# Attention row maxima per 128 queries: thin scores in four 32-row groups and one wide maximum, with compact reciprocals

## The chip, the cores and the metric

The kernel runs on one core of a Trainium2 chip. The metric is the device time of one execution in microseconds (us); lower is better. Engines are named as in the profile: PE is TensorE (PEld its weight loads), DVE is VectorE, ACT is ScalarE, POOL is GpSimd, SP is SyncE, whose queue here issues nearly all DMAs.

## The reference, cut to what matters

It is a transformer block with conditioning: two sequences of 2048 rows of 512 features, 16 heads of 32 features, an MLP of width 1024, all float32.

```
ada = silu(c) @ Wada + bada             # six shift / scale / gate rows per sequence
h = ln(x) * (1 + scale_msa) + shift_msa
q, k, v = h @ Wq + bq, h @ Wk + bk, h @ Wv + bv        # 16 heads of 32
A = softmax(q @ k.T / sqrt(32))         # per sequence and head: 2048 x 2048
x = x + gate_msa * ((A @ v) @ Wo + bo)
h2 = ln(x) * (1 + scale_mlp) + shift_mlp
out = x + gate_mlp * (gelu(h2 @ W1 + b1) @ W2 + b2)
```

The softmax needs, for each of the 2048 queries of a head, a number near the row's largest score to subtract before the exponential; any such number gives the same quotient.

## The kernel before, in words

There are three stages on one core: the first computes q, k and v for 8 chunks of 512 rows and writes them to DRAM; the second is attention, one head after another, 2 x 16 = 32 heads (numbered g = 0 to 31); the third is output projection and MLP, again by chunks. The change is in the second stage.

Products that need accuracy split each float32 number into a leading part (`hi`, rounded to the type float32r) and a remainder (`lo`). For the scores, 32 features of a head are stacked three times over 96 partitions: q as hi, hi, lo and k as hi, lo, hi, so one matmul over 96 rows gives hi·hi + hi·lo + lo·hi. These stacks are `qs[u]` and `ks[u]`. Row 96 (`M_ROW`) of `qs` carries minus the row maximum of each query, row 96 of `ks` ones, so a matmul over 97 rows gives scores less the maximum.

A head is worked in 16 steps (`NT`), step t for keys 128t to 128t+127. In one step PE computes the four pieces of transposed scores (128 keys x 512 queries, `scores`, line 1113), ACT exponentiates each (line 670) into `prob`, a ring of four steps, and PE then multiplies with v (`values`, line 1127: four column groups of 32, each an ordinary float32 matmul that stands as two instructions, hence x8 in the trace). The sums over the keys (the softmax's denominators) are made in two ways: the tiles in `POOL_TILES` are added up by POOL in halves of 1024 columns (line 538) into `psum_acc`; the others (`PE_TILES`, 5 of 16) and `psum_acc` at the end are summed by PE with a matrix of ones (`tile_sum`, `finish_denominators`, line 1118, x8 each). ACT copies the finished denominators of head g-1 out in step 1 of head g (line 650); DVE inverts them over 128 x 512 elements (line 874), scales the output (line 877), and SP stores it (line 398).

Between these, in a fixed order written out by hand (`FILLS_AT`, `SPREAD`), PE computes for the *next* head another 64 pieces of scores, queries on the partitions, 512 keys each, over 96 rows (`max_scores`, line 1104), in a ring of three PSUM banks; DVE takes the maximum of each (line 868) into `part_max`. After the 64th, DVE reduces the 64 columns to 16 (line 812), PE transposes them (line 1047), DVE negates them (line 818), and SP puts them into row 96 (`put_max`, line 391). The scores of the head use a second ring of three banks.

Each engine runs its list in order and waits on semaphores. In SP's list `stage2(g)` waits for the denominators of head g-1, loads q, k and v of head g+2 (`load_head`: seven DMAs of 256 KB, v last, in 2048 runs of 128 bytes), then `put_max(g+1)`, then `store_head(g-1)`. Three buffers (`NBUF`) hold q, k, v and output of a head. The first head's maxima are found in the first stage.

Of the kernel before, what the change touches and what calls it, by code (L numbers as in the profile page):

```python
# [19 lines left out]
F32 = mybir.dt.float32  # L20
# [5 lines left out]
P = 128  # L26
# [17 lines left out]
NBUF = 3  # L44
M_ROW = 3 * DH
POOL_TILES = [0, 1, 2, 3, 5, 6, 7, 9, 10, 11, 12]
# [4 lines left out]
FILLS_AT = (5, 5, 4, 4, 5, 4, 5, 4, 4, 5, 5, 4, 4, 4, 2, 0)  # L51

SPREAD = {0: (0, 0, 0, 0, 0), 2: (1, 1, 0, 0, 0), 4: (1, 1, 0, 1, 1), 5: (1, 1, 1, 1, 1)}
STEP_MAX = NT - 2
A_BANKS, B_BANKS = 3, 3
# [3 lines left out]
STEPS_SPLIT, STEP_PROJECT, STEP_ROOT, STEP_TRANSPOSE = (2, 4), 6, 10, 15  # L59
AHEAD = 3  # L60
COL = P // 4
LOADS = 7


def block_kernel(nc, x, cT, wq, wk, wv, wo, w1, w2, wada, bqT, bkT, b1T, badaT, bada, bv, bo, b2, out):
# [3 lines left out]
    att_dram = nc.dram_tensor("attention_T", [D, B * L], F32, kind="Internal").ap()  # L69

    with ExitStack() as ctx:
# [28 lines left out]
        qs = [view(acts_r, 4096 * u, L) for u in range(NBUF)]  # L100
        ks = [view(acts_r, 4096 * u + L, L) for u in range(NBUF)]

        oT_r = view(acts_r, 0, 2, KC, CH)
        g_r = view(acts_r, 4096, 4, 2, CH)
        h2T = view(acts_r, 8192, 2, KC, CH)
        assert [g % NBUF for g in range(G - 3, G)] == [2, 0, 1]
# [7 lines left out]
        v_sb = [view(work, at, NT, DH) for at in (512, 0, 1024)]  # L114
        o_st = [view(work, at, CH) for at in (2560, 3072, 1536)]
# [30 lines left out]
        row_max = sb("row_max", [P, NT])  # L146
        neg_max = sb("neg_max", [NT, P], F32R)
# [46 lines left out]
        ones_row = sem("ones_row")  # L194
        head_in = [sem(f"head_in{u}") for u in range(NBUF)]
        a_mm = sem("a_mm")
        a_max = sem("a_max")
        max_ok = sem("max_ok")
        maxT_mm = sem("maxT_mm")
        neg_ok = sem("neg_ok")  # L200
        neg_in = sem("neg_in")
# [6 lines left out]
        den_raw = sem("den_raw")  # L208
        rec_ok = sem("rec_ok")
        o_ok = sem("o_ok")  # L210
# [33 lines left out]
        def rows_of(w, c0):  # L244
# [8 lines left out]
                    for n, (w, at) in enumerate(((wq, stage[0]), (wk, stage[1]), (wv, as_piece(gate))))]  # L253
        w_pieces += [(w2[n * D:(n + 1) * D, :].rearrange("(k p) n -> p k n", p=P), stage[n],
                      [w2_r[:, s, n * KC:(n + 1) * KC, :] for s in range(2)]) for n in range(2)]
# [4 lines left out]
        LATE_STEP = 2  # L260
# [24 lines left out]
        def _(sp):  # L285
# [101 lines left out]

            def put_max(g, u):

                sp.wait_ge(neg_ok, g + 1)  # L390
                sp.dma_start(qs[u][M_ROW:M_ROW + 1, :].bitcast(F32),
                             neg_max[:].bitcast(F32)).then_inc(neg_in, 16)
# [23 lines left out]
            load_head(1, 1)  # L416
# [4 lines left out]
            for k, (rows, _) in enumerate(late):  # L421
# [6 lines left out]
                if k == 1:  # L428
                    sp.wait_ge(qkv_mm, NCHUNK * MM_CHUNK)
                    stored(NCHUNK)  # L430
                    load_head(2, 2)
            put_max(1, 1)
            with sp.Fori(0, G // NBUF - 1) as i:
                for k in range(1, NBUF + 1):
                    stage2(i * NBUF + k, k % NBUF, True)
# [19 lines left out]
            for g in range(G // NBUF * NBUF - NBUF + 1, G - 1):  # L455
                stage2(g, g % NBUF, g + 2 < G)
# [3 lines left out]
            load_x(0, 0, xc, xc_in)  # L460
            store_head(G - 2, (G - 2) % NBUF)
            load_first_oT(1)
# [31 lines left out]
        def _(pool):  # L494
# [14 lines left out]
            def row_of_ones(u):  # L509
                nc.gpsimd.memset(ks[u][M_ROW:M_ROW + 1, :].bitcast(F32), 1.0).then_inc(ones_row, 1)  # L510
                pool.wait_ge(ones_row, u + 1)

            row_of_ones(0)
# [8 lines left out]
            for u in range(1, NBUF):  # L522
                row_of_ones(u)
# [42 lines left out]
        def _(act):  # L566
# [91 lines left out]
            def probs(g, u, uses, prev, between={}):  # L658


                for t in range(NT):
# [6 lines left out]
                    for j in range(NQ):  # L668
                        act.wait_ge(b_mm, g * (NT * NQ) + t * NQ + j + 1)
                        nc.scalar.activation(prob[:, t % RING, j * CH:(j + 1) * CH], ps[:, A_BANKS + (u + t * NQ + j) % B_BANKS, :],  # L670
                                             ACT.Exp, scale=SCALE).then_inc(exp_ok, 1)
                    if prev and t == 0:
                        take_output(g - 1, (u + 2) % NBUF, uses)
# [8 lines left out]
            with act.Fori(0, G // NBUF) as i:  # L682
                for k in range(1, NBUF + 1):
                    probs(i * NBUF + k, k % NBUF, i, True)
            def split_first_oT(half):
# [39 lines left out]
        def _(dve):  # L725
            nc.vector.memset(cs_pad, 0.0).then_inc(pad_ok, 1)
            nc.vector.memset(ones[:], 1.0).then_inc(ones_ok, 1)
# [82 lines left out]
            def row_maxima(g):  # L810
                dve.wait_ge(a_max, (g + 1) * FILLS)
                nc.vector.tensor_reduce(row_max[:], part_max[:], AX.X, ALU.max).then_inc(max_ok, 1)

            def negate_max(g):
                dve.wait_ge(maxT_mm, g + 1)
                if not isinstance(g, int) or g:
                    dve.wait_ge(neg_in, g * 16)
                nc.vector.tensor_scalar(neg_max[:], ps[0:NT, 0, 0:P], -1.0, None, ALU.mult).then_inc(neg_ok, 1)
# [3 lines left out]
            def chunk(n, p, turn, nxt=True, nxt2=True, at=T_AT, ada={}, max_after={}, max_at=None):  # L822

                for m in range(MM_CHUNK):
                    for _ in range(max_after.get(m, 0)):
                        first_max(next(fills))
                    if m == max_at:
                        row_maxima(0)
                    take(n, m)
                    if m == max_at:  # L830
# [475 lines left out]
```

## Time and profile before

| | us |
|---|---|
| median of 3 runs (2633.13 to 2639.24) | 2637.26 |
| span of the profiled execution | 2625.2 |
| PE busy | 2543.3 (97%) |
| DVE busy | 1841.4 (70%) |
| POOL busy | 1625.0 (62%) |
| ACT busy | 1309.9 (50%) |

The page gives no time of the profiled execution beside its span; the median of the timed runs is 12.1 us above that span. Attention takes the stretch from about 420 to 2180 us. Busy time of PE counts from a matmul's start to its modelled end, and matmuls overlap, so PE's share is no measure of how much of its peak is used. The columns of the trace's answers are named where each group stands below.

### The profile page before, as it was taken

To read this page: it belongs to the slowest core of one execution; us is meant where nothing else is said; L and a number is where in the kernel's file an instruction comes from. 1 tells how busy PE (TensorE), PEld (TensorE's weight loads), DVE (VectorE), ACT (ScalarE), POOL (GpSimd) and SP (SyncE) were. 2 spreads that over 40 slices of the span, in tenths; PEclk is the share of its full clock that TensorE was granted. 3 is DMA by queue.
4 is the path that set the end of the run, shared out by engine and by line. 5 is a ranking of instruction groups with operands and counts; after the bars stand their busy time and mean duration, and the time that the engine had idled before them with its cause. 6 is when DMAs were issued, how large, how long until landed. Compare 5 with 4: busy or idle time off the path is not lost.

```text
span 2625.2 us, 45742 instructions
## 1 busy us (share of the span) xinstructions
PE 2543.3 (97%) x13208; PEld 1482.7 (56%) x13208; DVE 1841.4 (70%) x2872; ACT 1309.9 (50%) x2429; POOL 1625.0 (62%) x744
## 2 busy tenths in 40 slices
PE   7999899999999999999999999999999979999998
PEld 5788654444444444444444444444444437888887
DVE  5444588887877878778777787778778745555553
ACT  3333245665666656666666665666656642222221
POOL 0000157887888878888878888878888772112120
PEclk9999999999999999999999999999999989999999
DMA  7655631111211112211122111122111001121100
GB/s 263 207 192 167 153 112 49 33 34 39 60 34 33 33 38 56 40 33 33 35 44 56 33 33 35 35 52 46 33 34 33 21 25 53 49 73 71 48 32 32
DMA packets 141459, 163.15 MB, mean 62 GB/s; under 512 B 76048, under 2 KB 92944, under 8 KB 134032
## 3 DMA queue, kind: packets, MB, share of 16 engines
q1 hardware_dynamic: 140480, 159.95, 23.2%
q8 instruction: 129, 2.11, 0.3%
q14 instruction: 130, 1.06, 0.1%
q10 hardware_dynamic: 720, 0.02, 0.0%
HBM read 100.95 MB, written 58.72 MB: 61 GB/s over the span
## 4 chain that ended last, share of the span: by engine, by line
PE 93%; DVE 3%; issue 1%; ACT 1%; DMA 1%; SPq 0%; POOL 0%; ACTq 0%; POOLq 0%; DVEq 0%
PE ps L1113 21%; PE ps L1015 20%; PE ps L1104 19%; PE ps L1127 18%; PE ps L1118 7%; PE ps L1248 7%; DVE part_max L868 1%; PE ps L1024 1%; DVE weights_r L882 1%; PE ps L1059 1%; PE ps L1047 0%; DMA work<-v_rows 0%; DVE work L942 0%; ACT work L670 0%; DMA work<-in_x 0%
## 5 line engine op out<-in xcount | busy, mean ns | idle before, releaser
L538 POOL TENSOR_TENSOR work<-work 128x1024 f32<-128x1024 f32 x640 | 1505.7, 2395 | 296.7 <-PE ps L1118 262.7
L868 DVE TENSOR_REDUCE part_max<-ps 128x1 f32<-128x512 f32 x1984 | 1229.0, 682 | 321.3 <-PE ps L1104 320.7
L670 ACT ACTIVATE work<-ps 128x512 f32<-128x512 f32 x2048 | 1070.9, 602 | 697.3 <-PE ps L1113 697.2
L1113 PE MATMUL ps<-acts_r 97*128 97x512 f32 x2048 | 836.4, 418 | 26.0 <-ACT work L670 14.7
L1104 PE MATMUL ps<-acts_r 96*128 96x512 f32 x1984 | 811.3, 409 | 6.8 <-DVE part_max L868 6.7
L1113 PEld LDWEIGHTS ps<-acts_r 97*128 97x128 f32 x2048 | 383.1, 190 | 396.7 <-ACT work L670 308.4
L1127 PE MATMUL ps<-work 128*32 128x512 f32 x4096 | 545.3, 604 | 0.0
L1104 PEld LDWEIGHTS ps<-acts_r 96*128 96x128 f32 x1984 | 375.6, 189 | 263.0 <-DVE part_max L868 182.4
L1015 PE MATMUL ps<-acts_r,weights_r 128*128 128x512 f32 x1536 | 380.3, 397 | 5.7 <-DVE acts_r L790 5.7
L1015 PEld LDWEIGHTS ps<-acts_r,weights_r 128*128 128x128 f32 x1536 | 291.1, 191 | 69.3 <-issue 6.8
L547 POOL TENSOR_TENSOR work<-work,gate_b 128x512 f32<-128x512 f32 x60 | 84.5, 1439 | 214.3 <-DMA work<-in_x 172.8
L1127 PEld LDWEIGHTS ps<-work 128*32 128x32 f32 x4096 | 94.2, 109 | 203.2 <-issue 186.6
L1118 PE MATMUL ps<-work,ones 128*32 128x512 f32 x1536 | 206.4, 610 | 0.0
L505 POOL TENSOR_TENSOR var_eps<-var_eps,mv 128x4 f32<-128x4 f32 x16 | 3.2, 201 | 327.2 <-DVE mv L768 327.2
L713 ACT ACTIVATE work<-ps,b_sb 128x512 f32<-128x512 f32 x64 | 44.1, 690 | 309.7 <-PE ps L1015 309.6
L1248 PE MATMUL ps<-w_r,acts_r 128*128 128x512 f32 x768 | 184.5, 391 | 0.0
L1015 PE MATMUL ps<-weights_r,acts_r 128*128 128x512 f32 x768 | 183.6, 392 | 0.0
L1015 PEld LDWEIGHTS ps<-weights_r,acts_r 128*128 128x128 f32 x768 | 143.7, 188 | 36.9 <-issue 7.0
L1248 PEld LDWEIGHTS ps<-w_r,acts_r 128*128 128x128 f32 x768 | 143.0, 188 | 29.2 <-issue 0.2
L607 ACT ACTIVATE work<-ps,bq_sb 128x512 fp32r<-128x512 f32 x64 | 44.1, 689 | 206.3 <-PE ps L1015 170.9
L922 DVE CAST acts_r<-work 128x512 fp32r<-128x512 f32 x64 | 27.9, 436 | 128.6 <-ACT work L713 128.6
L874 DVE RECIPROCAL bv_rows<-bv_rows 128x512 f32<-128x512 f32 x32 | 106.6, 3331 | 8.0 <-ACT bv_rows L650 8.0
(69 smaller groups left out, 897.5 us busy)
## 6 DMA issues: line engine op xcount, KB each, us to landing
work<-in_x SPq DMA_DIRECT2D x16, 1024.0 KB, 5.4
acts_r<-q_hi SPq DMA_DIRECT2D x64, 256.0 KB, 4.8
acts_r<-k_hi SPq DMA_DIRECT2D x64, 256.0 KB, 6.4
q_hi<-work SPq DMA_DIRECT2D x32, 256.0 KB, 2.6
q_lo<-work SPq DMA_DIRECT2D x32, 256.0 KB, 3.3
k_hi<-work SPq DMA_DIRECT2D x32, 256.0 KB, 2.6
k_lo<-work SPq DMA_DIRECT2D x32, 256.0 KB, 3.2
v_rows<-work SPq DMA_DIRECT2D x32, 256.0 KB, 2.0
```

The lines of the kernel that those rows point to most:

```text
L538: nc.gpsimd.tensor_tensor(psum_acc[:, at], first, prob[:, t % RING, at], ALU.add).then_inc(add_ok, 1)
L547: nc.gpsimd.tensor_tensor(xc[b][:, t, :], xc[b][:, t, :], gate_b[:, which, b, :], ALU.add).then_inc(done, 1)
L607: nc.scalar.activation(qk_st[:, m % 2, 0, :].bitcast(F32R), ps[:, 2 + m % 4, :], ACT.Identity, bias=bq_sb[:, m // KC, m % KC:m % KC + 1]). ...
L670: nc.scalar.activation(prob[:, t % RING, j * CH:(j + 1) * CH], ps[:, A_BANKS + (u + t * NQ + j) % B_BANKS, :], ACT.Exp, scale=SCALE).then_ ...
L868: nc.vector.tensor_reduce(part_max[:, f // NQ, f % NQ:f % NQ + 1], ps[:, (u + f) % A_BANKS, :], AX.X, ALU.max).then_inc(a_max, 1)
L874: nc.vector.reciprocal(recip[:], recip[:]).then_inc(rec_ok, 1)
L1015: mm = nc.tensor.matmul(o, lhs(s, kk), rhs(r, kk), start=(kk == 0 and s == r), stop=(kk == KC - 1 and s == 1))
L1104: nc.tensor.matmul(ps[:, (u + f) % A_BANKS, :], qs[u][0:M_ROW, f // NQ * P:(f // NQ + 1) * P], ks[u][0:M_ROW, j * CH:(j + 1) * CH], start= ...
L1113: nc.tensor.matmul(ps[:, A_BANKS + (u + t * NQ + j) % B_BANKS, :], ks[u][0:M_ROW + 1, t * P:(t + 1) * P], qs[u][0:M_ROW + 1, j * CH:(j + 1 ...
L1118: mm = nc.tensor.matmul(ps[j * DH:(j + 1) * DH, DEN_BANK, :], ones[:, 0:DH], src(j), start=first, stop=last)
L1127: mm = nc.tensor.matmul(ps[j * DH:(j + 1) * DH, O_BANK, :], v_sb[u][:, t, :], prob[:, t % RING, j * CH:(j + 1) * CH], start=(t == 0), stop ...
L1248: mm = nc.tensor.matmul(ps[:, 4 + t, :], g_r[:, f % 4, s, t * P:(t + 1) * P], w2_r[:, r, f, :], start=(f == 0 and s == r), stop=(f == FB - ...
```

## The change

In words:

- The maximum is taken of hi·hi alone (over 32 rows instead of 96). The 32 rows of q's leading part are loaded four times, into partitions 0-31, 32-63, 64-95 and 96-127 (`qm`), and a quarter of the keys into each (`km`). For 128 queries (a block b), PE issues four matmuls of 32 rows, one per row group, into four PSUM banks (`block_scores`), and DVE takes one maximum over all 2048 columns (`block_max`). There are 16 blocks per head; block t+2 of the next head is issued in step t (`MAX_LEAD` 2). The four banks are one buffer: PE waits for the maximum of block b before it writes block b+1. The scores keep two banks instead of three.
- The 16 columns of maxima are transposed by DVE (32 x 32 blocks), without PE and without a negation (row 96 of `ks` is now minus one); `put_max` takes four DMAs.
- The denominators: SP spreads one row of each quarter to 128 x 16 elements, DVE inverts these, SP writes them to DRAM and reads them back, broadcast to 32 partitions for each quarter. DVE inverts in step 5 and scales the output in step 9 of the next head.
- SP's `stage2` now waits for head g-1's denominators, loads head g+1 (seven DMAs) and then `qm`, `km` of head g+2 (`load_max`, eight DMAs: 4 x 256 KB and 4 x 64 KB), then does the spreading, the store, and `put_max`. Two buffers instead of three.
- POOL adds 9 tiles instead of 11; PE sums 7 instead of 5.
- The order of a step on PE: two scores, the block of maxima, two scores, values of the step before, its tile sum. The last 128 rows of W2 are loaded at the end of attention (their place holds `km`). In the last head the projection starts at step 7 instead of 6.

The core of the diff (`load_max`, `spread_reciprocals` and `stage2` are in SP's list; `transpose_max` to the first `head` in DVE's; `block_scores` and the loop over the steps in PE's):

```diff
-NBUF = 3
+NBUF = 2
-POOL_TILES = [0, 1, 2, 3, 5, 6, 7, 9, 10, 11, 12]
+POOL_TILES = [0, 1, 2, 4, 5, 7, 9, 10, 12]
-A_BANKS, B_BANKS = 3, 3
+MAX_LEAD = 2
+FIRST_PAIRS = (4, 9)
+A_BANKS, B_BANKS = 4, 2
+STEP_RECIP, STEP_SCALE = 5, 9
...
+            def load_max(g, u):
+                r = bass.ds(g * DH, DH)
+                for j in range(NQ):
+                    at = slice(j * DH, (j + 1) * DH)
+                    sp.dma_start(qm[u][at, :].bitcast(F32), qk_hi[0][r, :]).then_inc(max_in[u], 16)
+                    sp.dma_start(km[u][at, :].bitcast(F32), qk_hi[1][r, j * CH:(j + 1) * CH]).then_inc(max_in[u], 16)
...
+            def spread_reciprocals(g):
+                sp.wait_ge(den_raw, g + 1)
+                for j in range(NQ):
+                    sp.dma_start(den_c[j * DH:(j + 1) * DH, :], recip[j * DH:j * DH + 1, :].rearrange("o (p c) -> o p c", c=NT)).then_inc(den_in, 16)
+                sp.wait_ge(rec_ok, g + 1)
+                sp.dma_start(rec_dram.rearrange("(p c) -> p c", c=NT), den_c[:]).then_inc(rec_out, 16)
+                sp.wait_ge(rec_out, g * 16 + 16)
+                for j in range(NQ):
+                    sp.dma_start(recip[j * DH:(j + 1) * DH, :],
+                                 rec_dram[j * CH:(j + 1) * CH].rearrange("(o c) -> o c", o=1).broadcast_to((DH, CH))).then_inc(rec_in, 16)
...
-            def stage2(g, u, load):
-                if load:
-                    sp.wait_ge(den_mm, START + g)
-                    load_head(g + 2, (u + 2) % NBUF)
-                put_max(g + 1, (u + 1) % NBUF)
-                store_head(g - 1, (u + 2) % NBUF)
+            def stage2(g, u, more=True):
+                sp.wait_ge(den_mm, START + g)
+                load_head(g + 1, 1 - u)
+                if more:
+                    load_max(g + 2, u)
+                spread_reciprocals(g - 1)
+                store_head(g - 1, 1 - u)
+                put_max(g + 1, 1 - u)
...
+            def transpose_max(g):
+                if not isinstance(g, int) or g:
+                    dve.wait_ge(m_max, g * NT)
+                    dve.wait_ge(maxT_in, g * (16 * MAX_PIECES))
+                nc.vector.transpose(max_T[:], row_max[:]).then_inc(maxT_ok, 1)
+            def block_max(g, b):
+                if b == 0:
+                    dve.wait_ge(maxT_ok, g)
+                dve.wait_ge(m_mm, (g - 1) * NT + b + 1)
+                nc.vector.tensor_reduce(row_max[:, b:b + 1], ps[:, 0:A_BANKS, :].rearrange("p j n -> p (j n)"), AX.X, ALU.max).then_inc(m_max, 1)
+            def small_reciprocals(g):
+                dve.wait_ge(den_in, g * (16 * NQ) + 16 * NQ)
+                nc.vector.reciprocal(den_c[:], den_c[:]).then_inc(rec_ok, 1)
+            def scale_output(g, u):
+                dve.wait_ge(rec_in, g * (16 * NQ) + 16 * NQ)
+                dve.wait_ge(o_raw, g + 1)
+                nc.vector.tensor_tensor(o_st[u], o_st[u], recip[:], ALU.mult).then_inc(o_ok, 1)
+            def head(g, u, nxt=True, more=True):
+                for t in range(NT):
+                    if t == STEP_RECIP:
+                        small_reciprocals(g - 1)
+                    if t == STEP_SCALE:
+                        scale_output(g - 1, 1 - u)
+                    if nxt and t + MAX_LEAD < NT:
+                        block_max(g + 1, t + MAX_LEAD)
+                    if nxt and t + MAX_LEAD == NT - 1:
+                        transpose_max(g + 1)
+                    if more and t + MAX_LEAD >= NT:
+                        block_max(g + 2, t + MAX_LEAD - NT)
...
+            def block_scores(g, u, b):
+                if not isinstance(g, int) or g > 1 or b:
+                    pe.wait_ge(m_max, (g - 1) * NT + b)
+                for j in range(NQ):
+                    at = slice(j * DH, (j + 1) * DH)
+                    mm = nc.tensor.matmul(ps[:, j, :], qm[u][at, b * P:(b + 1) * P], km[u][at, :], start=True, stop=True)
+                mm.then_inc(m_mm, 1)
...
+                for t in range(NT):
                     scores(g, u, t, 0)
                     scores(g, u, t, 1)
                     if t in between:
                         between[t]()
                     scores(g, u, t, 2)
                     scores(g, u, t, 3)
+                    if t:
+                        values(g, u, t - 1)
+                        if t - 1 in PE_TILES:
+                            tile_sum(g, t - 1)
+                    elif loads is not None:
+                        last_values(g - 1, 1 - u)
+                    if t == 1 and loads is not None:
+                        finish_denominators(g - 1)
```

## Rows read from the trace of the kernel before

**Rows 1.** The page, busy us, share of the span, instructions of each engine.

```profile
PE 2543.3 (97%) x13208; PEld 1482.7 (56%) x13208; DVE 1841.4 (70%) x2872; ACT 1309.9 (50%) x2429; POOL 1625.0 (62%) x744
```

**Rows 2.** Chain of waits through one head, 1087.7 to 1143.9 us: its shares by line.

```profile
by line: PE ps L1113 31.8%; PE ps L1104 28.8%; PE ps L1127 27.4%; PE ps L1118 10.4%; issue 1.7%; PE ps L1047 0.6%
```

**Rows 3.** Timeline, DVE: start us, duration us; the reciprocals of heads 0 and 29.

```profile
477.76 3.33 DVE L874 RECIPROCAL bv_rows<-bv_rows 128x512 f32<-128x512 f32 x1
...
2088.73 3.33 DVE L874 RECIPROCAL bv_rows<-bv_rows 128x512 f32<-128x512 f32 x1
```

**Rows 4.** Timeline, PE, two steps inside a head: start us, duration us, count.

```profile
1097.82 1.06 PE L1118 MATMUL ps<-work,ones 128*32 128x512 f32 x8
1098.70 1.04 PE L1127 MATMUL ps<-work 128*32 128x512 f32 x8
1099.68 0.50 PE L1104 MATMUL ps<-acts_r 96*128 96x512 f32 x1
1100.01 0.40 PE L1113 MATMUL ps<-acts_r 97*128 97x512 f32 x1
...
1101.66 0.40 PE L1104 MATMUL ps<-acts_r 96*128 96x512 f32 x1
1101.99 1.06 PE L1127 MATMUL ps<-work 128*32 128x512 f32 x8
1102.99 0.50 PE L1113 MATMUL ps<-acts_r 97*128 97x512 f32 x1
1103.33 0.39 PE L1104 MATMUL ps<-acts_r 96*128 96x512 f32 x1
```

**Rows 5.** The page, weight loads: busy us, mean ns of one.

```profile
L1104 PEld LDWEIGHTS ps<-acts_r 96*128 96x128 f32 x1984 | 375.6, 189 | 263.0 <-DVE part_max L868 182.4
L1127 PEld LDWEIGHTS ps<-work 128*32 128x32 f32 x4096 | 94.2, 109 | 203.2 <-issue 186.6
```

**Rows 6.** Timeline, DVE, the same head.

```profile
1091.17 0.69 DVE L877 TENSOR_TENSOR work<-work,bv_rows 128x512 f32<-128x512 f32 x1
1103.75 2.48 DVE L868 TENSOR_REDUCE part_max<-ps 128x1 f32<-128x512 f32 x4 [0.47 <-PE ps L1104]
1142.69 0.22 DVE L812 TENSOR_REDUCE row_max<-part_max 128x16 f32<-128x64 f32 x1
```

**Rows 7.** Groups by line, 1000 to 1520 us: busy us, mean ns of one.

```profile
L868 DVE TENSOR_REDUCE part_max<-ps 128x1 f32<-128x512 f32 x604 | 374.1, 683 | 97.4 <-PE ps L1104 97.2
```

**Rows 8.** Timelines, ACT and POOL, the same head.

```profile
1103.52 2.07 ACT L670 ACTIVATE work<-ps 128x512 f32<-128x512 f32 x4 [0.52 <-PE ps L1113]
...
1099.09 47.04 POOL L538 TENSOR_TENSOR work<-work 128x1024 f32<-128x1024 f32 x20 [9.08 <-PE ps L1118]
```

**Rows 9.** Timeline, SP's queue: first and last of `load_head`'s seven issues.

```profile
1099.11 0.35 SPq L384 DMA_DIRECT2D acts_r<-q_hi  x1
...
1101.96 0.39 SPq L386 DMA_DIRECT2D work<-v_rows  x1
```

**Rows 10.** DMA issues 1099 to 1112 us: KB, us from issue to landing.

```profile
work<-v_rows SPq DMA_DIRECT2D x1, 256.0 KB, 8.8
```

**Rows 11.** Busy us by engine and stretch; then PE's clock (1.00 is full), DMA share, GB/s.

```profile
1100.00:1108.50 8.50, 8.50 (x45) 4.68 (x47) 7.25 (x12) 6.54 (x13) 8.37 (x4) 1.00 1.03 210
```

**Rows 12.** Timeline, SP's queue, first stage: a store issued right behind a `load_head`.

```profile
312.50 0.43 SPq L386 DMA_DIRECT2D work<-v_rows  x1
313.70 6.24 SPq L335 DMA_DIRECT2D q_hi<-work  x1
```

**Rows 13.** Line 335, the stores of q and k: issue to landing.

```profile
DMA to landing us min/median/max: 2.4/2.6/10.0
```

**Rows 14.** Timeline, PE, at the start of another head.

```profile
1592.13 0.63 PE L1113 MATMUL ps<-acts_r 97*128 97x512 f32 x1 [1.56 <-issue]
...
1593.97 1.92 PE L1127 MATMUL ps<-work 128*32 128x512 f32 x8
```

**Rows 15.** Stretch of rows 14: columns as in rows 11.

```profile
1592.20:1595.50 3.30, 3.30 (x12) 1.37 (x16) 1.38 (x2) 1.19 (x2) 0.00 (x0) 0.52 0.32 72
```

More of the change, by code:

```diff
@@ L415, in _ @@
             sp.wait_ge(qkv_mm, (NCHUNK - 1) * MM_CHUNK)
-            load_head(1, 1)
+            load_max(1, 1)
+            load_max(2, 0)
             store_qk(NCHUNK - 1, *ORDER[NCHUNK - 1])
@@ L681, in _ @@
                 act.wait_ge(v_out[i], START + 16 * NCHUNK * TT // 2)
-            with act.Fori(0, G // NBUF) as i:
+            with act.Fori(0, LOOPS) as i:
                 for k in range(1, NBUF + 1):
                     probs(i * NBUF + k, k % NBUF, i, True)
+            for g in (G - 3, G - 2):
+                probs(g, g % NBUF, (g - 1) // NBUF, True)
+            act.wait_ge(last_in, 16)
+            act.wait_ge(m_mm, (G - 1) * NT)
+            nc.scalar.activation(w2_r[:, 0, FB - 1, :], tmp3[:, 0, :], ACT.Copy).then_inc(last_hi, 1)
             def split_first_oT(half):
@@ L1146, in last_values, with head @@
                     tile_sum(g, NT - 1)
[L1148 to L1161 removed]
+            def head(g, u, loads=None, between={}):
+                if loads is not None:
+                    pe.wait_ge(head_in[u], loads * (16 * LOADS))
                 for t in range(NT):
                     scores(g, u, t, 0)
[L1165 removed]
                     scores(g, u, t, 1)
[L1167 to L1176 removed]
                     if t in between:
@@ new lines, in head, with next_blocks, ahead @@
+                    if t == 1 and loads is not None:
+                        finish_denominators(g - 1)
+            def next_blocks(g, u, more):
+                def ahead(t):
+                    b = t + MAX_LEAD
+                    if b < NT:
+                        block_scores(g + 1, 1 - u, b)
+                    elif more is not None:
+                        if b == NT:
+                            pe.wait_ge(max_in[u], more * (16 * MAX_LOADS))
+                        block_scores(g + 2, u, b - NT)
+                return {t: lambda t=t: ahead(t) for t in range(NT)}
@@ new lines, in _, with first_blocks @@
+            pe.wait_ge(minus_row, 1)
+            pe.wait_ge(v_ok, START + NCHUNK * TT)
+            pe.wait_ge(max_in[1], 16 * MAX_LOADS)
+            order = iter([(1, 1, b) for b in range(NT)] + [(2, 0, b) for b in range(MAX_LEAD)])
+            def first_blocks(t):
+                for _ in range(2 if t in FIRST_PAIRS else 1):
+                    h, u, b = next(order)
+                    if (h, b) == (2, 0):
+                        pe.wait_ge(max_in[0], 16 * MAX_LOADS)
+                    block_scores(h, u, b)
@@ L1193, in _ @@
+            head(0, 0, between={t: lambda t=t: first_blocks(t) for t in range(NT)})
+            assert next(order, None) is None
+            pe.wait_ge(minus_row, NBUF)
             nc.disable_value_cache = True
-            with pe.Fori(0, G // NBUF) as i:
+            with pe.Fori(0, LOOPS) as i:
                 for k in range(1, NBUF + 1):
-                    head(i * NBUF + k, k % NBUF, i + 1 if k + 1 < NBUF else i + 2, True, True)
+                    head(i * NBUF + k, k % NBUF, i + 1 if k == 1 else i + 2, next_blocks(i * NBUF + k, k % NBUF, i + 2))
```

193 lines of the change are left out of this document (88 added, 105 removed).

## The prediction

> **What bounds the kernel now.** I read the page first: PE is busy 97% of the span, DVE 70%, POOL 62%, ACT 50% [rows 1]. Then the chain of waits through one head: every piece of it but 1.7% is PE work, the scores and the maxima's scores about 30% each, values 27%, sums 10% [rows 2]. So attention runs at PE's pace, and a head's price is read from PE's timeline. The reciprocals give the period: those of heads 0 and 29 start 1610.97 us apart, over 29 heads, 55.55 us a head [rows 3].
>
> Inside a step [rows 4], matmuls over 96 or 97 rows start 0.236 us apart (1100.01 to 1101.66, seven of them). Where PE goes from these to the column groups of `values` the next start comes 0.33 later, and the first matmul after a `values` takes 0.34. `values` with what surrounds it costs 1.00 (1101.99 to 1102.99), a sum beside it 0.87 more (1097.82 to 1099.68 for both). An ordinary step is eight matmuls and a `values`, about 3.07.
>
> **The new step on PE.** Removed: four matmuls at 0.236 (0.94 a step). Added: four matmuls of 32 rows in other row groups, and two changes of array shape in place of none. No row of before shows a matmul in a row group. The weight loads of 128 columns take 189 ns and those of 32 columns 109 [rows 5]: 0.83 ns a column, so a load of 128 columns holds the weight path for 0.107 us. Hidden behind a stream of 0.236 that costs nothing, but four matmuls that run side by side each bring such a load. I take the loads one after another and the matmuls side by side: the last of the four starts 0.10 + 3 x 0.107 = 0.42 after the block begins and ends 0.40 later, at 0.82. Bounds: all at once, ending at 0.50 (the length of a first matmul in rows 4); all in turn, 0.50 + 3 x 0.236 = 1.21. I am nearest to the loads' row. For the changes of shape I take the 0.33 that rows 4 show.
>
> With the first score at 0: second 0.34, block 0.67, its last matmul 1.09, third score 1.42, fourth 1.76, values 2.09, next step 3.09. So the new block saves PE nothing (3.09 against 3.07). A step with a sum takes 3.96. There are eight of those: seven tiles (3, 6, 8, 11, 13, 14, 15), whose sums fall into steps 4, 7, 9, 12, 14, 15 and 0, and the finish in step 1. Two sums more than before are 1.7 us a head.
>
> **The loop of block and maximum.** DVE takes 2.48 us for four pieces of 512 [rows 6] and 683 ns for one [rows 7]; 64 columns take 0.22. That is 0.15 fixed and 1.04 ns a column, so 2.28 us for 2048. The four banks are one buffer, so PE's next block waits for this maximum and the maximum waits for the block. From a matmul's end to DVE's start is 0.03 (1103.33 + 0.39, then 1103.75 [rows 4, 6]); I take as much for the way back. The loop is 0.82 + 0.03 + 2.28 + 0.03 = 3.16, longer than the plain step's 3.09. The wait sits in PE's list ahead of two scores, the values and everything behind them, and ACT waits for these. A period is thus 8 x 3.96 + 8 x 3.16 = 57.0 us, with no help from a quick step for a slow one, since nothing is buffered.
>
> **What lies beside it, at no cost.** The old reciprocal (3.33), transposition and negation were in DVE's list; the new DVE extras (0.69 to scale [rows 6], about 0.25 and 0.2 for the inversion of 16 columns and the transposition, bounds 0.15 and 0.69 from rows 6) fall into the 0.88 in which DVE waits for a block; without that cover they cost 1.2 a head. Two score banks: exponential 0 ends at 0.50 + 0.03 + 0.60 = 1.13 (the 0.60 and a pitch of 0.49 from rows 8), before the third score at 1.42; exponential 1 ends at 1.62, before 1.76. If blocks cost nothing, the banks would set in instead, so this is thin cover. POOL: 16 adds at 2.35 are 38 us of 57 [rows 8]. The maxima's row: the last block of a head is issued in step 13, 10.3 us before the next head; maximum 3.1, transposition 0.2, four issues at 0.5 [rows 9], landing 2.6 (the ordinary store in rows 13) are 8.0. So the wait at the head's start, 1.56 in rows 14, goes; it is within the 55.55.
>
> **SP's queue and the reciprocals: the term that decides.** Call T0 the end of the finish in step 1 of head g; in rows 4 that is about 1098.82. SP then issues `load_head`, seven DMAs 0.47 apart [rows 9]; v lands 8.8 after its issue [rows 10], at 1110.76 or T0 + 11.9. While they run, the DMA engines are full (share 1.03) at 210 GB/s [rows 11]. So they are limited by the engines, and what is queued behind them comes after. Behind them the change puts `load_max`: 4 x 256 KB + 4 x 64 KB = 1.31 MB, 6.2 us at 210 GB/s, done at T0 + 18.1. Only then come the four small DMAs that spread the denominators, T0 + 18.3, although the denominators are there at about T0 + 0.7. That SP's DMAs queue like this is in the first stage: the store issued right behind a `load_head` held SP's queue for 6.24 us [rows 12], and the stores land in 2.6 as a rule but 10.0 at most [rows 13].
>
> DVE's inversion stands before the maximum of step 5. Blocks of steps 2, 3, 4 begin at T0 + 0.67, 3.83, 6.99, that of step 5 at 10.95, and its maximum would start at 11.80. DVE reaches the inversion at 10.12 and waits to 18.3; with 0.25 and two hops that maximum starts at 18.6. Everything moves by 6.8 us: PE does what does not need it and then stands at the block of step 6, with scores, values and ACT behind. Lower bound 0 (the small DMAs pass the large ones: 15 issues of 0.47, four more and 1.8 to 2.6 to land, T0 + 11.5, which costs almost nothing); upper bound 8, if SP's stalled queue leaves gaps between v and `load_max`. I take 6.8. The way on to the scaling in step 9 (a write, a read back, each 2 to 3 us) has over 10 us of steps and adds nothing.
>
> A stand of PE of 5 to 6 us has a second price. After a stand of 1.56 us (and one before it) PE ran at a granted clock of 0.52 [rows 14, 15], the 1.2 GHz level, with `values` 1.92 long instead of 1.06. Such a stretch costs up to 1.7 us; part of it falls into the stand. Bounds 0 and 1.7; I take 1.0 a head.
>
> **Sum.** 57.0 + 6.8 + 1.0 - 55.55 = 9.25 us a head. `load_max` is in 29 of the heads (1 to 29): 268 us. The first head (18 blocks at the loop's pace), head 30 and the last (two more sums, a later projection, W2's last piece, the denominators behind the load of x): +7, bounds -10 and +20. Together +275: the profiled span 2625 becomes 2900. The runs' median is 12.1 above that span; I add the change to the median: 2912 us.
>
> **A rule that says otherwise.** The block's price is the open one: by the rows, 0.42 to the last start. The Trainium skill, "TensorE: Matmul & The Clock Gate", Part 3 (packing small matmuls), gives 3.07 times the throughput for four row tiles of 32 rows and 512 columns. As an estimate from that page, the four would hold PE 0.94 / 3.07 = 0.31 instead of my 0.56, and the sum would be 2825 us with the wait for the denominators, still slower. No row here shows it.
>
> **Rivals.**
> - *Blocks truly side by side, the wait stays.* Block ends at 0.50: loop 2.84, long step 3.64, period 51.8. The maximum of step 5 would start at 10.5, so the wait is 8.1. 51.8 + 8.1 + 1.0 - 55.55 = 5.35 a head: 2637 + 155 + 7 = 2799. For it: column groups do run side by side (eight instructions in 1.00). Against: each of these loads only 32 columns.
> - *Faster: no wait for the denominators, blocks side by side.* One mechanism: the scores for the maxima cost PE a quarter. Period 51.8, 3.75 less a head: 2637 - 109 + 7 = 2535. It decides only if the spread denominators land before about T0 + 14, so the small DMAs must pass the large ones. Rows 12 and 13 speak against it.
> - *No wait, loads in turn.* 57.0 - 55.55: 2637 + 42 + 7 = 2686.
> - *Blocks in turn.* If row groups do not overlap: loop 3.55, long step 4.35, period 63.2, wait 5.2: 13.85 a head, 3046.
> - *The gain and the losses cancel.* Overlapping blocks with half the wait: near 2637.
>
> **Chances.** Forecast 55% (own range 2850 to 2960), blocks side by side with the wait 16%, faster 15%, no wait with loads in turn 6%, blocks in turn 5%, cancelled 3%. The range 2690 to 2990 leaves out the faster and the blocks in turn. The least that a measurement tells from no change is about 0.2% (5 us). Faster 0.15, same 0.03, slower 0.82.
>
> **What the changed profile would show.** DVE's small reciprocal waits for a DMA, 8 us a head; without that, the main term is wrong. PE's longest wait is for the wide maximum, once a head for over 5 us, with the granted clock down behind it. A wide maximum takes 2.28. From a block's first start to its last 0.3 to 0.4 (zero would be side by side). DVE idles 0.8 to 0.9 before each maximum. Steps with a sum are 0.8 longer than the others. The stretch at the head's start holds no wait. Total DMA traffic grows by about 40 MB. I am wrong if a head's period is under 60 us.

## The result, and the profile after

The changed kernel takes 2927.01 us (median of 4 runs, 2925.07 to 2928.84) against 2638.25 beside it on the same chip: ratio 1.1105, 95% interval 1.1089 to 1.1122. The 2638.25 is a median of four runs, one of which was a slow one of 3602.26; the ratio leaves that one out, and the other three have the median 2637.26. The forecast was 2912 in a range from 2690 to 2990, with 0.82 on slower. The profiled run took 2925.07 in all, its span is 2923.3 at a mean granted clock of 0.946.

From the page of the kernel after: busy time by engine, then three groups of section 5 (busy and mean ns of one, then the idle time ahead of them and what ended it).

```profile
PE 2642.9 (90%) x13656; PEld 1235.5 (42%) x13656; DVE 1633.5 (56%) x1355; ACT 1361.0 (47%) x2430; POOL 1316.7 (45%) x615
L880 DVE TENSOR_REDUCE row_max<-ps 128x1 f32<-128x2048 f32 x496 | 1134.7, 2288 | 601.9 <-PE ps L1186 601.9
L925 DVE RECIPROCAL den_c<-den_c 128x16 f32<-128x16 f32 x31 | 7.8, 253 | 236.6 <-DMA den_c<-bv_rows 236.6
L1186 PEld LDWEIGHTS ps<-w_r,acts_r 32*128 32x128 f32 x1984 | 98.9, 189 | 376.4 <-DVE row_max L880 268.4
```

PE fell from 97% busy [rows 1] to 90%: it now waits. DVE's work fell, as meant, and the time did not. The third line names a wait that the kernel before does not have, and the waits of the whole kernel after give its count and longest (total, times, longest):

```profile
DVE den_c L925 <- DMA den_c<-bv_rows: 236.6, 30, 8.6
```

That is 7.9 us in each of 30 heads. What precedes it is on SP's queue, and what follows it on DVE and PE. The kernel after, one head; first SP's queue (start, length):

```profile
1095.69 0.39 SPq L403 DMA_DIRECT2D work<-v_rows  x1
1096.31 5.19 SPq L410 DMA_DIRECT2D acts_r<-q_hi  x1
...
1104.56 0.32 SPq L411 DMA_DIRECT2D w_r<-k_hi  x1
1104.99 2.45 SPq L424 DMA_DIRECT2D den_c<-bv_rows  x4
```

The first DMA of `load_max`, behind the one for v, holds the queue for 5.19 us. The four small DMAs are issued at 1104.99, 12.2 us after `load_head` began (1092.79), although ACT had copied the denominators out by 1093.20. DVE in the same head (idle before, and what ended it):

```profile
1099.97 2.29 DVE L880 TENSOR_REDUCE row_max<-ps 128x1 f32<-128x2048 f32 x1 [0.80 <-PE ps L1186]
1110.26 0.25 DVE L925 RECIPROCAL den_c<-den_c 128x16 f32<-128x16 f32 x1 [8.00 <-DMA den_c<-bv_rows]
1110.43 2.23 DVE L880 TENSOR_REDUCE row_max<-ps 128x1 f32<-128x2048 f32 x1
```

The inversion lasts 0.25 us and waits for 8.00. Its maximum had its block ready at 1103.87 and starts at 1110.43. And PE:

```profile
1103.36 0.51 PE L1186 MATMUL ps<-w_r,acts_r 32*128 32x512 f32 x4
...
1105.80 0.73 PE L1195 MATMUL ps<-acts_r 97*128 97x512 f32 x2
1112.71 0.80 PE L1186 MATMUL ps<-w_r,acts_r 32*128 32x512 f32 x4 [6.18 <-DVE row_max L880]
1114.59 1.94 PE L1209 MATMUL ps<-work 128*32 128x512 f32 x8
```

PE stands for 6.18 us before the block of step 6; `values` after it takes 1.94 us. The stretch behind the stand in the windows view of PE (length, busy of PE, PEld, DVE, ACT and POOL, granted clock, DMA share, GB/s):

```profile
1112.70:1123.00 10.30, 10.29 (x38) 2.89 (x38) 4.58 (x2) 3.26 (x6) 4.45 (x2) 0.50 0.09 25
```

A granted clock of 0.50 is the 1.2 GHz level, for over 10 us after the stand; in the 6.18 us of the stand itself the mean is 0.73. This head has one of the longest such stretches. Over heads 1 to 29 the granted clock is 0.93 on average, which is, as an estimate from that mean, some 9 us a head at the lower level; before the change it is 1.00, with one stretch, at one head's start [rows 15].

From the first score of a head to that of the next is 65.54 us on average over 29 heads, against 55.55. 29 x 9.99 = 289.7 of the 298.1 us by which the spans differ.

### The profile page after: what moved, and what is told of

Read it like the earlier page. It is cut to its first block, busy times and chain, and to the rows that moved or that the text cites. A ratio compares the mean times of both kernels' runs of the same rounds, so it can differ in the third digit from the quotient of the medians.

```text
span 2923.3 us, 42275 instructions
## 1 busy us (share of the span) xinstructions
PE 2642.9 (90%) x13656; PEld 1235.5 (42%) x13656; DVE 1633.5 (56%) x1355; ACT 1361.0 (47%) x2430; POOL 1316.7 (45%) x615
## 2 busy tenths in 40 slices
DMA packets 172677, 210.50 MB, mean 72 GB/s; under 512 B 96016, under 2 KB 112400, under 8 KB 161424
## 4 chain that ended last, share of the span: by engine, by line
PE 70%; SPq 14%; DMA 5%; issue 4%; DVE 4%; ACT 2%; ACTq 0%; POOL 0%; DVEq 0%; POOLq 0%
PE ps L1195 20%; PE ps L1099 17%; PE ps L1209 14%; SPq L410 7%; PE ps L1200 7%; PE ps L1340 6%; PE ps L1186 5%; DMA den_c<-bv_rows 3%; DVE row_max L880 3%; SPq L424 2%; SPq L411 2%; ACT work L717 2%; SPq L402 1%; SPq L401 1%; PE ps L1108 1%
## 5 line engine op out<-in xcount | busy, mean ns | idle before, releaser
L585 POOL TENSOR_TENSOR work<-work 128x1024 f32<-128x1024 f32 x512 | 1200.6, 2375 | 895.5 <-PE ps L1200 527.9
L717 ACT ACTIVATE work<-ps 128x512 f32<-128x512 f32 x2048 | 1112.6, 595 | 865.8 <-PE ps L1195 820.2
L880 DVE TENSOR_REDUCE row_max<-ps 128x1 f32<-128x2048 f32 x496 | 1134.7, 2288 | 601.9 <-PE ps L1186 601.9
L1195 PE MATMUL ps<-acts_r 97*128 97x512 f32 x2048 | 903.3, 490 | 46.9 <-ACT work L717 32.0
L1195 PEld LDWEIGHTS ps<-acts_r 97*128 97x128 f32 x2048 | 355.4, 196 | 813.4 <-ACT work L717 540.3
L1209 PE MATMUL ps<-work 128*32 128x512 f32 x4096 | 583.3, 643 | 0.0
L1186 PE MATMUL ps<-w_r,acts_r 32*128 32x512 f32 x1984 | 262.7, 518 | 186.4 <-DVE row_max L880 186.3
L1200 PE MATMUL ps<-work,ones 128*32 128x512 f32 x2048 | 274.7, 609 | 0.0
L1186 PEld LDWEIGHTS ps<-w_r,acts_r 32*128 32x128 f32 x1984 | 98.9, 189 | 376.4 <-DVE row_max L880 268.4
L1200 PEld LDWEIGHTS ps<-work,ones 128*32 128x32 f32 x2048 | 68.0, 113 | 161.2 <-issue 161.2
```

The costliest lines, as they stand in the source:

```text
L585: nc.gpsimd.tensor_tensor(psum_acc[:, at], first, prob[:, t % RING, at], ALU.add).then_inc(add_ok, 1)
L880: nc.vector.tensor_reduce(row_max[:, b:b + 1], ps[:, 0:A_BANKS, :].rearrange("p j n -> p (j n)"), AX.X, ALU.max).then_inc(m_max, 1)
L1186: mm = nc.tensor.matmul(ps[:, j, :], qm[u][at, b * P:(b + 1) * P], km[u][at, :], start=True, stop=True)
L1195: nc.tensor.matmul(ps[:, A_BANKS + (t * NQ + j) % B_BANKS, :], ks[u][0:M_ROW + 1, t * P:(t + 1) * P], qs[u][0:M_ROW + 1, j * CH:(j + 1) * ...
L1200: mm = nc.tensor.matmul(ps[j * DH:(j + 1) * DH, DEN_BANK, :], ones[:, 0:DH], src(j), start=first, stop=last)
L1209: mm = nc.tensor.matmul(ps[j * DH:(j + 1) * DH, O_BANK, :], v_sb[u][:, t, :], prob[:, t % RING, j * CH:(j + 1) * CH], start=(t == 0), stop ...
```

## Experiments

All of them start from the changed kernel (called "after"). My theory: the wait of the inversion costs about 7 to 8 us a head, the rest is PE's longer step. The rivals: the shape of the blocks, the number of banks, or DVE's load is what costs.

**Denominators spread ahead of the loads.** The four small DMAs go to the front of SP's list; all else stays.

```
+    spread_denominators(g - 1)     # the wait and the four den_c DMAs
     load_head(...); load_max(...)
-    spread_reciprocals(g - 1)
+    spread_reciprocals(g - 1, False)   # the write and the reads back
```


> The changed kernel, with the four small DMAs that spread the denominators issued ahead of load_head and load_max instead of behind them. The changed kernel's steps sum to 56.7 us a head without the steps in which PE stands or runs at the lower clock, and to 65.5 with them; 8.9 us a head over 29 heads hang on the wait of the small reciprocal. Theory (the small DMAs queue behind 3 MB of loads): the wait of the small reciprocal for its DMA goes from 8 us a head to about 0, PE's clock stays up in attention, the head takes 56.7 us and the time is 2927 - 29 x 8.9 = about 2670 us. Rival (the spreading itself is slow, whatever its place): the wait stays at 7 to 8 us and the time near 2927.

Measured: 2678.61 us, ratio to before 1.0169 (1.0149 to 1.0189). The wait of the inversion is gone from the waits; a head takes 57.17. So the place of four small DMAs in one queue is worth 248 us of the 289, the granted clock in these heads is 1.00 again, and what is left of the change is still 1.7% slower than before.

**The steps moved instead.** The queue stays as it is; inversion and scaling come later.

```
-STEP_RECIP, STEP_SCALE = 5, 9
+STEP_RECIP, STEP_SCALE = 8, 11
```


> The changed kernel with DVE's inversion in step 8 instead of 5 and the scaling in step 11 instead of 9; SP's order as in the changed kernel. Theory (the denominators land about 18 us after the finish, DVE reaches step 8 about 20 us after it): no wait, as in e1, about 2670 us, though the DMAs land as late as before. Rival (DVE's wait is not what holds PE, or the chain to the scaling and the maxima's row becomes late instead): 2750 or more, with a new wait at the head's start.

Measured: 2692.03 us (one run), a head 57.42, and no wait for the denominators. So it is not the late data that costs, but a waiting instruction in DVE's list ahead of a maximum. Some 7 of the 13 us to the first experiment are in the heads (29 x 0.25): step 12 lasts 4.45 us, behind a scaling that took 2.01 instead of 0.69 beside one of POOL's additions. The rest I did not place.

**The spread between the two loads.**

```
 load_head(...)
+spread_denominators(g - 1)
 load_max(...)
```


> The changed kernel with the small DMAs between load_head and load_max. Theory (a queue in order): the denominators land right behind v, 12.3 us after the finish; DVE waits 2.2 us a head for them, the maximum of step 5 moves by 1.3 us, too short a stand to bring the clock down: 2670 + 29 x 1.3 = about 2708 us. Rival (the DMA engines share themselves out among all that is queued, so only the total of the loads counts, not the place): the wait stays near 8 us, 2900 us or more.

Measured: 2693.54 us (one run). The waits of this kernel:

```profile
DVE den_c L931 <- DMA den_c<-bv_rows: 77.0, 30, 3.8
```

2.6 us a head remain of 7.9, and step 6 is 3.63 us on average instead of 3.10. Behind `load_head` alone the denominators are a little late, behind both loads by much: it is `load_max` that made most of the wait, 233 of the 248 us.

**All blocks in one row group.** On top of the first experiment.

```
-  matmul(ps[:, j, :], qm[u][at, b * P:(b + 1) * P], km[u][at, :])
+  matmul(ps[:, j, :], qm[u][0:DH, b * P:(b + 1) * P], km[u][0:DH, :])
```


> e1 with all four matmuls of a block in the same row group of 32 (the maximum is then taken four times over the first quarter of the keys; the other three quarters are left out). Theory (in four row groups they run side by side, 0.01 us apart; in one they run in turn, 0.236 apart): the block's last start moves by 0.70, of which the wait for a score bank hid 0.2 to 0.3; plain step 3.48, step with a sum 4.35, 62.6 us a head, e1 + 173 = about 2843 us. Rival (what limits a block is its change of shape and the loads of 128 columns, not the row groups): e1 within 30 us.

Measured: 2870.58 us (one run), a head 63.14, and the maximum covers a quarter of the keys. PE's timeline:

```profile
1136.22 0.73 PE L1201 MATMUL ps<-acts_r 97*128 97x512 f32 x2
1136.88 1.19 PE L1192 MATMUL ps<-w_r,acts_r 32*128 32x512 f32 x4
1138.01 0.73 PE L1201 MATMUL ps<-acts_r 97*128 97x512 f32 x2
```

A block takes 1.19 us instead of 0.51. The four row groups do run side by side, and 192 us hang on it. The plain step is 3.44 to 3.57 us.

**Three banks for the scores.** The scores have three banks. A block has three matmuls, and its maximum covers three quarters of the keys (1536 columns instead of 2048). On top of the first experiment.

```
-A_BANKS, B_BANKS = 4, 2
+A_BANKS, B_BANKS = 3, 3
+BANK = (0, 1, 2, 0)
```


> e1 with three score banks instead of two and blocks of three matmuls in three banks (the maximum is over three quarters of the keys; the last quarter is left out of it). Theory (the two score banks set the plain step of 3.10: the fourth score waits for the second exponential, 1.65 after the step's start): the fourth score follows the third at 0.34 instead of 0.49, plain step 2.85 and step with a sum 3.7, head 57.2 - 16 x 0.25 = 53.2 us, time 2679 - 29 x 4.0 = about 2563 us. Rival (the block's matmuls and changes of shape set it): one matmul less in a block of 0.01 spacing brings nothing, 2670 or more.

Measured: 2850.36 us (one run), so the forecast of 2563 is far off, and yet the point it tested holds: a plain step is 2.77 us (3.10), one with a sum 3.61 (3.96). But three things changed at once, and the shorter maximum also shortens the loop with DVE; what speaks for the banks is read from PE's timeline under the last experiment. The loss begins in one place, the scaling of the output in step 9. This kernel's DVE:

```profile
1145.68 7.27 DVE L937 TENSOR_TENSOR work<-work,bv_rows 128x512 f32<-128x512 f32 x1 [2.61 <-DMA bv_rows<-reciprocals]
```

7.27 us for an operation of 0.69 [rows 6]. The maximum of step 10 stands behind it, PE stands for 7.46, and step 10 lasts 11.95. The two steps behind it take 4.18 and 4.71 on average instead of 2.77 and 3.61: the granted clock over these heads is 0.89. This opened a second question: what holds the scaling?

**More of the additions on POOL.** Eleven tiles instead of nine, on top of the first experiment; meant to take two sums from PE.

```
+POOL_TILES = [0, 1, 2, 3, 5, 6, 7, 9, 10, 11, 12]
```


> e1 with the 11 POOL tiles of the kernel before (PE sums 5 tiles instead of 7). Theory (a sum costs PE 0.86 and nothing hides it): 57.2 - 1.7 = 55.5 us a head, 2679 - 29 x 1.7 = about 2628 us, level with the kernel before. Rival (POOL's 20 additions of 2.35 are late for the ring of four steps, ACT waits for them): 2650 or more with ACT's wait for POOL.

Measured: 3033.4 us, ratio 1.1521 (1.1502 to 1.154), a miss by 405. Its DVE and POOL (a POOL row is a run of additions without a pause):

```profile
1217.59 11.98 DVE L936 TENSOR_TENSOR work<-work,bv_rows 128x512 f32<-128x512 f32 x1 [0.70 <-DMA bv_rows<-reciprocals]
```

```profile
1194.08 34.94 POOL L591 TENSOR_TENSOR work<-work 128x1024 f32<-128x1024 f32 x15 [14.28 <-PE ps L1206]
```

POOL's run ends at 1229.02, DVE's operation at 1229.57. It lasts until POOL's run ends, as long as five of them take. And the run ends because the stall has reached its own supply: the next maximum stands behind DVE's operation, PE's block behind the maximum, ACT behind PE, and POOL's next addition waits for ACT.

```profile
1234.63 2.36 POOL L591 TENSOR_TENSOR work<-work 128x1024 f32<-128x1024 f32 x1 [5.61 <-ACT work L723]
```

In the kernel of the first experiment the same operation comes in a pause of POOL's:

```profile
1129.00 23.34 POOL L591 TENSOR_TENSOR work<-work 128x1024 f32<-128x1024 f32 x10 [17.30 <-PE ps L1206]
1153.99 9.38 POOL L591 TENSOR_TENSOR work<-work 128x1024 f32<-128x1024 f32 x4 [1.65 <-ACT work L723]
```

```profile
1152.58 0.69 DVE L936 TENSOR_TENSOR work<-work,bv_rows 128x512 f32<-128x512 f32 x1
```

**The order of scores, block and values.** On top of the eleven tiles: both score pairs together, then the block.

```
-  between[t]()
   scores(g, u, t, 2); scores(g, u, t, 3)
...
+  scores(g, u, t, 2); scores(g, u, t, 3); between[t]()
```


> e6 with the values and sums of the step before between the two pairs of scores and the block after the second pair. Theory (the third score's and fourth score's waits for their banks fall into the values; what stays is the first score's wait for the third exponential behind the block): plain step 3.0 instead of 3.10, 55.5 - 1.6 = 53.9 us a head, about 2580 us, 2% under the kernel before. Rival (the wait for a bank moves from the fourth score to the next step's first two, 2 x 1.16 us of bank for four pieces whatever the order): no more than 10 us from e6.

Measured: 3026.48 us, ratio 1.1507 (1.1486 to 1.1528). The plain step stays 3.10 where the theory had 3.0, and the time is 7 us from that of the eleven tiles: the rival holds. As a cycle this order has the same neighbours as the other, and the pair of scores behind the block still starts 0.49 us apart; it is now the next step's first pair.

**Three banks and eleven tiles together.** The short diffs of both.

> e5 with the 11 POOL tiles of the kernel before (the last quarter of the keys is left out of the maximum, as in e5). Theory: both gains add, 53.2 - 1.7 = 51.5 us a head, about 2513 us. Rival: POOL's 47 us of additions no longer fit the ring at steps of 2.85, ACT waits, 2540 or more.

Measured: 2936.5 us (one run), steps 2.77 and 3.61, scaling 11.63: the same stall.

**A pause of POOL's for the scaling.** On top of the eleven tiles, POOL waits before its addition 5 of a head until the scaling is done.

```
+  if k == POOL_PAUSE and not (isinstance(g, int) and g == G - 1):
+      pool.wait_ge(o_ok, START + g)
```


> e6 with one wait more in POOL's list: before its sixth tile addition of a head it waits until DVE has scaled the output of the head before. In e6 that scaling took 12.0 us instead of 0.69, from the landing of its DMA until the end of POOL's unbroken run of additions. Theory (a DVE operation with two SBUF operands can't run while POOL's additions follow one another, and gets in when POOL pauses): the scaling takes 0.7 again, POOL's pause costs it 1 us of the 8 it has free, the head takes 57.2 - 1.7 = 55.5 us, time about 2628 us, level with the kernel before. Rival (POOL's additions for 11 tiles are too long for the ring of four steps in this order): the scaling is short and ACT waits for POOL instead, 2660 or more.

Measured: 2651.67 us, ratio 1.0072 (1.0053 to 1.0092), a head 55.88. DVE's and POOL's rows:

```profile
1246.54 0.69 DVE L939 TENSOR_TENSOR work<-work,bv_rows 128x512 f32<-128x512 f32 x1 [0.84 <-DMA bv_rows<-reciprocals]
```

```profile
1222.93 23.36 POOL L594 TENSOR_TENSOR work<-work 128x1024 f32<-128x1024 f32 x10 [7.95 <-PE ps L1209]
1247.48 23.37 POOL L594 TENSOR_TENSOR work<-work 128x1024 f32<-128x1024 f32 x10 [1.20 <-DVE work L939]
```

One wait of 1.20 us on POOL gives back 382 us, and the granted clock in these heads goes from 0.89 to 1.00. That POOL's additions hold the scaling is shown by this. The forecast of 2628 is missed by 24 us: the rival's sign is there as well, ACT waits for POOL 56 times, 113.3 us in all.

**A scaling of 16 columns.** On the eleven tiles without the pause, `o_st[u][:, 0:16]` times `recip[:, 0:16]` in place of 512 columns.

> e6 with the scaling cut to 16 of 512 columns (the rest of the output stays unscaled, so this part is left out). Theory (DVE is shut out as long as POOL's run lasts, whatever its own size): it still takes 11 to 12 us, time near 3030. Rival (both read at once and share the rate, so the time goes with the columns): 0.7 us or less, time near 2630.

Measured: 3027.01 us (one run). Its group on the page:

```profile
L936 DVE TENSOR_TENSOR work<-work,bv_rows 128x16 f32<-128x16 f32 x31 | 341.7, 11022 | 22.1 <-DMA bv_rows<-reciprocals 22.1
```

11.02 us on average for 16 columns, against 11.58 for 512. In each of heads 1 to 29 the operation ends 0.03 to 0.04 us after an addition of POOL's with 16 columns, and 0.55 after one with 512. So DVE isn't slowed column by column; it is shut out, and then does its work at once.

**Three banks, eleven tiles, the pause, the scaling in step 10.**

> e5 (three score banks, blocks of three matmuls; the last quarter of the keys is left out of the maximum) with the 11 POOL tiles of the kernel before, the pause of e9, and the scaling in step 10. In e5 and e12 the scaling met POOL's run too (7 us and more); their plain step was 2.77 and their step with a sum 3.61. Theory (two score banks were the plain step's limit, and the scaling's stand hid the gain): 10 x 2.77 + 6 x 3.61 = 49.4 us a head, POOL's 47 us and its pause just beside it, so 49.4 to 51: 2628 - 29 x 5.3 = about 2475 us. Rival (POOL's additions become the bound): 2520 or more, with ACT's wait for POOL in the list of waits.

Measured: 2665.66 us, ratio 1.0116 (1.0088 to 1.0143), a head 57.37 where the forecast of 2475 had 49.4 to 51. The steps are 2.77 and 3.61 up to step 10, the stall of the scaling is gone, and POOL sets in, as in the rival. The waits of this kernel:

```profile
ACT work L727 <- POOL work L595: 114.2, 37, 5.7
```

Twenty additions and the pause are more than these heads give POOL time for. In step 11 ACT waits for it and PE stands, 2.49 us in the head I read, and over the 10 us behind that stand the granted clock is 0.52. So the short stand costs twice: step 11 is 3.4 us longer than a plain one, and steps 12 to 15 together another 4.3, mostly at the lower clock.

**The same with nine tiles.** The short diff against the kernel with three banks: the pause as above, and

```
-STEP_RECIP, STEP_SCALE = 5, 9
+STEP_RECIP, STEP_SCALE = 5, 10
```


> e13 with the changed kernel's 9 POOL tiles instead of 11 (the last quarter of the keys is left out of the maximum, as in e5). In e13 POOL's 20 additions and the two stands around them took the whole head and ACT's ring waited for them. With 9 tiles POOL has 38 us of work. Theory (two score banks were the limit of the plain step, POOL e13's): plain step 2.77, step with a sum 3.61, eight of each, 51.0 us a head against 55.55, time 2634 - 29 x 4.5 = about 2502 us, 5% under the kernel before. Rival (the scaling's chain of DMAs, which lands no earlier than about 31 us into the head, still delays DVE or POOL): 2550 or more.

Measured: 2499.16 us (2496.97 to 2500.28), ratio 0.9492 (0.9476 to 0.9507), a head 51.31: faster than both kernels, with PE at 97%. PE's timeline of a plain step, to the next one's first score (2.77 us):

```profile
1131.68 0.73 PE L1207 MATMUL ps<-acts_r 97*128 97x512 f32 x2
1132.34 0.50 PE L1196 MATMUL ps<-w_r,acts_r 32*128 32x512 f32 x3
1132.77 0.73 PE L1207 MATMUL ps<-acts_r 97*128 97x512 f32 x2
1133.43 1.07 PE L1221 MATMUL ps<-work 128*32 128x512 f32 x8
1134.45 0.74 PE L1207 MATMUL ps<-acts_r 97*128 97x512 f32 x2
```

The third and fourth score start 0.33 apart here, and 0.49 with two banks (0.73 and 0.99 for the pair): that is the bank. The change's idea pays here, with PE neither short of a bank nor in a loop with DVE. How much of the gain from 3.10 is the bank and how much the shorter block and maximum, these runs don't part. It takes a maximum over fewer keys. The number that is subtracted cancels in the softmax and only guards the exponential's range, so whether that is allowed is a question of the data, not of the chip; a version with the whole maximum and three score banks wasn't tried.

## Why the prediction was right, and where not

**The wait for the denominators: right.** Predicted: the spread lands 18.3 us after the finish of step 1, and the maximum of step 5 moves by 6.8. Measured: the spread lands 17.7 us after the finish (1110.26 and 1092.53), and the maximum would have started at 1103.89 and did at 1110.43: 6.5. The parts hold too: the queue blocks behind v (5.19 us), and the small DMAs land behind the 1.31 MB. The first experiment takes this term out: 65.54 - 57.17 = 8.37 us a head, the shift and 1.8 more.

**The clock: right in kind, too small.** I took 1.0 us a head between 0 and 1.7; what the shift leaves of the 8.37 is 1.8, just above my bound. That is a remainder and not a measurement of the clock alone. My bound came from a stretch of 3.3 us at the lower level; in the head shown there are 10.3 us of it behind the stand.

**The step with a sum: right in number.** 3.96 predicted, 3.96 measured; and the maximum of 2048 columns takes 2.29 (2.28), with 0.81 idle before it (0.88). The 3.96 is luck of the same kind as the plain step's, told below: it was added up with a block that was too long and without the waits for banks. With three banks the same step is 3.61.

**The block: the step that failed.** "I take the loads one after another and the matmuls side by side" gave 0.82 us; a block takes 0.51, its four matmuls start 0.003 to 0.004 apart. Rows 5's time of a load of 128 columns was right (189 ns), but not what I made of it, a path that passes one load at a time. The rule of the Trainium skill, "TensorE: Matmul & The Clock Gate", Part 3, has 3.07 times for four row tiles. Here it is 1.19 / 0.51 = 2.3 times, from first start to last end, between that and the 1.21 / 0.82 = 1.5 of my terms. The loop of block and maximum is therefore 0.51 + 2.29 and two hops of 0.03, 2.86 us and not 3.16. By my own rival that should have given steps of 3.64 and 2.84 and 2799 us.

**Two score banks: the second error, of the other sign.** I had put them among what costs nothing, "thin cover", to set in "if blocks cost nothing". They cost little enough. PE's weight loads in a plain step of the kernel after (start, length, idle before and releaser):

```profile
1134.39 0.19 PEld L1195 LDWEIGHTS ps<-acts_r 97*128 97x128 f32 x1 [0.33 <-ACT work L717]
1134.88 0.19 PEld L1195 LDWEIGHTS ps<-acts_r 97*128 97x128 f32 x1 [0.30 <-ACT work L717]
```

The third score waits for exponential 0 and the fourth for exponential 1, 0.49 us apart (ACT's pitch in rows 8) where PE could do them 0.24 to 0.34 apart. That makes 3.10 of a step that PE and the loop with DVE would do in 2.86, as an estimate from these terms; three banks, with a block of three matmuls, show 2.77. DVE's idle time of 0.81 in the kernel after is this wait handed on: in the forecast it was the block's own length. So a step of 3.10 came out beside a forecast of 3.16 by two errors of 0.3 us that cancel. The rival "blocks truly side by side, the wait stays" had the right block and the wrong step, for the same reason.

**DVE's extras at no cost: right for this kernel, by luck of place.** The scaling took 0.68 (DVE, kernel after):

```profile
1126.47 0.68 DVE L930 TENSOR_TENSOR work<-work,bv_rows 128x512 f32<-128x512 f32 x1
```

The cover was not only the 0.88 us of DVE that I named but also a pause of POOL's, which stood from 1123.22 to 1127.95. Where a step is 0.3 us shorter or POOL has two tiles more, it costs 7 to 12 us a head.

**The sum.** By my terms: 57.0 + 6.8 + 1.0 = 64.8 us a head; measured, with the clock as the remainder: 57.2 + 6.5 + 1.8 = 65.5. The steps are within 0.2, the shift is 0.3 less, the clock is 0.8 more. The 0.74 that remain, times 29, are 21.5 of the 23.3 us by which the span exceeds the 2900 of the forecast. The median exceeds it by only 15, because it lies 3.7 above the profiled span and not 12.1 as before. The DMA traffic grew by 47.35 MB (210.50 after, 163.15 before), not 40; I did not follow the rest.

## What to carry to other kernels

Before DMAs are put into a queue, ask who is behind them there: four DMAs of 2 KB behind 3.15 MB of loads cost 248 of 2927 us here, nearly all of it by the last 1.3 MB, and moving the wait in the engine's list took away nearly as much as moving the DMAs in the queue's. A short operation placed ahead of a link of the critical loop is priced by what it waits for, not by its length. When one part of a loop gets faster, recompute every buffer's turnaround: here the gain of the row groups lay behind two banks, and behind these in a lock with another engine, and only with all three out of the way, and a maximum over three quarters of the keys, did the kernel become faster. A short stand inside a busy stretch has a second price where the clock falls behind it: read the granted clock of the stretch that follows, not the stand alone.

## What the runs showed of the hardware

- DVE's multiplication of two SBUF operands is shut out while POOL runs SBUF additions back to back: 11.98 us beside five additions, 11.02 on average even for 16 columns, 0.69 with POOL paused. The Trainium skill, "SBUF — State Buffer", section "SBUF: two separate sides", has the two share a port pair under a lock that is held for a whole instruction. If DVE got the pair as soon as an addition ends, it would wait for one at most, 2.35 us. The kernel with late steps agrees (2.01 us, in after one addition), the one with eleven tiles does not. Why DVE gets its turn after one addition in the one and waits for the end of the run in the other stays open. That POOL's next operands were ready doesn't part them: in the kernel with late steps the operand of the addition ahead of which DVE got in was ready 2.0 us before that addition's start, in the one with three banks 2.2 us before one ahead of which DVE did not get in.
- Four fp32r matmuls of 32 rows and 512 columns in four row groups, each with a load of 128 columns, take 0.51 us from first start to last end; in one row group 1.19.
- A DMA issued behind a whole `load_head` held SP's queue for 5.19 us, and small DMAs behind both loads landed 17.1 us after their data was there (1110.26 and 1093.20).
- A stand of PE of 6.18 us brought a granted clock of 0.50 for the 10.3 us behind it, though PE was busy before and after; over all heads of that kernel the mean is 0.93. With three banks, eleven tiles and the pause a stand of 2.49 us was followed by 10 us at 0.52, while heads with stands of 0.75 us on average (the pause alone on the eleven tiles) kept 1.00.
